# Filters by row halves, context by head columns, one output product per chunk, and statistics between normalisations in a four-layer kernel

## The chip, the cores and the metric

One core of one Trainium2 chip runs the whole program. The metric is device microseconds (us) of one execution. TensorE is PE in the rows, VectorE is DVE, ScalarE is ACT, GpSimd is POOL, and SyncE, which here only issues DMAs, is SP.

## What is computed

The input x is (32, 16, 16, 32) in fp32: 32 images of 256 tokens with 32 channels. Four blocks follow each other. Each adds a token mixer and then a second mixer to x, each behind a layer norm over the 32 channels. Cut to what the change touches:

```python
# block 0: linear attention, 4 heads of 32
q = softmax(q, over the 32 channels of a head) / sqrt(32)
k = softmax(k, over the 256 tokens)
context = einsum('bnhd,bnhe->bhde', k, v / 256)
x = x + layernorm(einsum('bhde,bnhd->bnhe', context, q) @ w_out + b_out) * ln_scale
# block 0: spectral unit (STU): causal convolution over tokens with 16 filters phi,
# weights M_phi_plus and M_phi_minus (the latter with alternating signs), scaled by sigma**0.25,
# plus three direct taps M_u, for four sequence lengths, weighted by a gumbel softmax
x = x + stu(layernorm(x))
# block 1: triangle update
a = sigmoid((x @ Wa1 + ba1) * (x @ Wa2 + ba2)); b likewise
x = x + sigmoid(x @ Wg + bg) * (layernorm(einsum('bikc,bkjc->bijc', a, b)) @ Wz + bz)
# blocks 1 and 3: recurrent cell behind a batch normalisation of Wx
x = x + scan(y = sigmoid(batchnorm(x @ W.T) + y @ V.T))
# blocks 2 and 3: row scan with a width-9 convolution; block 2: mixture of 16 experts, top 8
```

## The kernel before, in words

Channels of four images fill the 128 partitions (`NQ` = 4 groups of `C` = 32). The free axis holds `G` = 8 images of `T` = 256 tokens, 2048 columns, which are worked in `CH` = 4 chunks of 512 columns (`BANK`), the width of one of the eight PSUM banks. Everything is fp32, and a matmul leaves two records in the trace. Every engine has its own program, written out by hand in the order in which it runs, and counting semaphores tie them together: `wait_ge(S(name), n)` holds the engine and everything behind it. `keep_busy(n, k)` on PE issues n matmuls of 512 columns whose results nobody reads.

**Layer norm** (`ln_centre`, `ln_square`, `ln_spread`, `ln_rstd`): PE subtracts the mean (L197), ACT squares (L256), PE averages the squares (L203), ACT takes Ln and Exp (L262, L267), and DVE multiplies (L281, L1142, L1242, L1326). `ln_pe` interleaves the chunks.

**Attention** runs over U = 16 units, a chunk j and a group q each. Its loops are software pipelines. On PE, turn i issues `attn_proj(i)` (k and q, 512 columns each, and v, four matmuls of 128 columns), `attn_mid(i-1)` (four transposes, L567), one call of `filters` if there is one, `attn_ctx(i-2)` (four matmuls 128x128 of 128 columns, L578), `attn_out(i-3)` (two matmuls of 256 columns onto the 32 partitions of group q) and a second call of `filters`. `filters(m)` makes two columns e of the STU's filters, from a strided weight of 128 rows, 256 columns each, into bank 1; there are 16 calls, two each in turns 5 to 12 (`FILT_FROM` = 5). It waits until ACT has copied the call before (`filt_sb`). On DVE, turn i does `v_k(i)` (maximum, L1093), `v_q(i)` (L1100, L1102, L1106), `v_qw(i-1)` (L1111, L1113, L1116) and `v_ctx(i-2)` (L1121 and four small multiplications on L1129, one for each head, since only the diagonal blocks of the 128x128 product are wanted). ACT does `a_k(i)` (L910), `a_kn(i-1)` (L931), a copy of filters (L939), `a_v(i)` (L919), `a_q(i)` (L925), another copy of filters, and `a_y` (L935) when a chunk's four groups are out. POOL multiplies q by its weight (L457). Only when all 16 units are through does the layer norm of the output start. k alternates between banks 0 and 5.

**STU**: SP's DMAs spread the filters over `toep`, then PE convolves (L622). `add_stu(j)` adds a bank to x in 16 small steps (L1165), which also turn token-major rows into channel groups.

**Triangle**: `twice` writes the normalised x into `xm` in token order and into `xnH` in row order. PE takes columns of both as weights: `xnH[:, m]` is contiguous, `xmQ[:, :, m]` has a stride of 16 elements. Then DVE adds biases (L1198) and multiplies (L1203), ACT takes the sigmoids (L978, L982) and, with DVE, spreads `a` over a block diagonal (L987, L1208), and PE multiplies (L687). `add_triangle` brings the result back.

**Recurrent cells** (`rnn(0, 4)` and `rnn(1, 8)`): PE makes Wx per chunk (`wx`), then `BUSY_BN[0]` = 3 unread matmuls, then waits for `bn_mean_in`. DVE writes the guessed state with four memsets (L1253, L1254), takes four batch statistics (L1258) and aggregates them (L1259).

## Time and profile before

| | |
|---|---|
| median of 3 runs | 501.35 us (499.7 to 503.72) |
| the profiled execution's own time | 500.5 us |
| its span, first to last instruction | 498.7 us |
| mean granted clock of TensorE, share of full | 0.974 |
| PE busy | 460.4 us (92%) |
| weight loads | 290.6 us (58%) |
| DVE busy | 264.7 us (53%) |
| ACT busy | 180.4 us (36%) |
| POOL busy | 32.6 us (7%) |

The span is one execution recorded by the hardware profiler. Busy shares are averages over the stages: attention (about 23 to 137 us), its STU (to 267), the triangle (to 309), the first cell (to 346), row scan, experts and row scan (to 462), the second cell and the store (to 499). Matmul records overlap, so a stage with PE at 99% is bound by PE's order of issue and not by its peak.

### The profile page before, as it was taken

To read this page: it belongs to the slowest core of one execution; us is meant where nothing else is said; L and a number is where in the kernel's file an instruction comes from. 1 tells how busy PE (TensorE), PEld (TensorE's weight loads), DVE (VectorE), ACT (ScalarE), POOL (GpSimd) and SP (SyncE) were. 2 spreads that over 40 slices of the span, in tenths; PEclk is the share of its full clock that TensorE was granted. 3 is DMA by queue.
4 is the path that set the end of the run, shared out by engine and by line. 5 is a ranking of instruction groups with operands and counts; after the bars stand their busy time and mean duration, and the time that the engine had idled before them with its cause. 6 is when DMAs were issued, how large, how long until landed. Compare 5 with 4: busy or idle time off the path is not lost.

```text
span 498.7 us, 6421 instructions
## 1 busy us (share of the span) xinstructions
PE 460.4 (92%) x2488; PEld 290.6 (58%) x2488; DVE 264.7 (53%) x566; ACT 180.4 (36%) x362; POOL 32.6 (7%) x32
## 2 busy tenths in 40 slices
PE   6999999998879999998998998998999899999991
PEld 2456677765327476753764855485475575475490
DVE  3599878787579140105105645646533736633745
ACT  1785766663650000001002272454504510504360
POOL 0135221123000000000000000000000000000000
PEclk8999999998999999999999999998999988999996
DMA  9300000059940000000002000000000000000003
GB/s 276 152 2 1 1 0 1 1 128 224 197 85 0 2 0 0 1 0 0 1 2 41 1 1 1 1 1 2 0 1 2 1 0 1 0 2 1 0 1 85
DMA packets 6506, 15.20 MB, mean 30 GB/s; under 512 B 2619, under 2 KB 5323, under 8 KB 5707
## 3 DMA queue, kind: packets, MB, share of 16 engines
q1 hardware_dynamic: 5899, 14.25, 11.7%
q10 hardware_dynamic: 576, 0.52, 0.3%
q8 instruction: 20, 0.33, 0.3%
q14 instruction: 11, 0.09, 0.1%
HBM read 5.86 MB, written 1.05 MB: 14 GB/s over the span
## 4 chain that ended last, share of the span: by engine, by line
PE 67%; DVE 19%; ACT 8%; issue 4%; DMA 1%; POOLq 0%; SPq 0%; DVEq 0%; ACTq 0%
PE bank L510 22%; PE bank L622 19%; PE bank L791 5%; PE bank L203 5%; PE bank L736 3%; PE bank L747 3%; PE bank L197 3%; DVE xQ L1165 2%; ACT lnv L262 2%; PE bank L219 2%; PE bank L578 1%; ACT rs L267 1%; DVE attn_scratch L1129 1%; ACT sq L256 1%; DVE xn L249 1%
## 5 line engine op out<-in xcount | busy, mean ns | idle before, releaser
L622 PE MATMUL bank<-xn,arena 128*128 128x512 f32 (+15 forms) x332 | 88.9, 427 | 2.4 <-DVE xn L249 2.4
L622 PEld LDWEIGHTS bank<-xn,arena 128*128 128x128 f32 x332 | 56.3, 190 | 36.0 <-issue 27.0
L256 ACT ACTIVATE sq<-bank 128x512 f32<-128x512 f32 x36 | 21.3, 591 | 119.5 <-PE bank L197 98.6
L510 PE MATMUL bank<-sb_consts 128*128 128x512 f32 (+1 forms) x140 | 62.5, 571 | 0.0
L1165 DVE TENSOR_TENSOR xQ<-bank,xQ 32x128 f32<-32x128 f32 x64 | 24.5, 382 | 33.1 <-PE bank L656 18.0
L203 PE MATMUL bank<-sq,sb_consts 128*128 128x512 f32 x72 | 38.4, 615 | 0.9
L510 PEld LDWEIGHTS bank<-sb_consts 128*128 128x128 f32 x140 | 25.3, 194 | 23.3 <-issue 23.1
L262 ACT ACTIVATE lnv<-bank 128x512 f32<-128x512 f32 x36 | 21.5, 598 | 33.6 <-PE bank L203 33.6
L510 PE MATMUL bank<-xn,sb_w_attn 128*128 128x512 f32 x64 | 31.1, 604 | 0.6 <-DVE attn_scratch L1106 0.5
L1174 DVE TENSOR_TENSOR arena<-bank,rs 128x512 f32<-128x512 f32 x4 | 2.8, 692 | 51.7 <-ACT rs L267 51.7
L791 PEld LDWEIGHTS bank<-arena,sb_w_late 128*128 128x128 f32 x180 | 23.0, 191 | 11.1 <-DVE arena L1332 8.0
L791 PE MATMUL bank<-arena,sb_w_late 128*128 128x128 f32 x180 | 27.2, 287 | 1.7 <-DVE arena L1332 1.3
L736 PE MATMUL bank<-arena,sb_consts 128*128 128x128 f32 x144 | 27.7, 276 | 0.7 <-DVE arena L1282 0.7
L747 PE MATMUL bank<-arena,sb_w_late 128*128 128x128 f32 x144 | 27.9, 276 | 0.0
L197 PE MATMUL bank<-xQ,sb_consts 128*128 128x512 f32 x40 | 22.0, 643 | 6.2 <-DVE xQ L1165 3.3
L203 PEld LDWEIGHTS bank<-sq,sb_consts 128*128 128x128 f32 x72 | 12.1, 190 | 22.6 <-ACT sq L256 11.5
L1016 ACT ACTIVATE arena<-bank 128x128 f32<-128x128 f32 x72 | 20.0, 278 | 14.0 <-PE bank L747 13.8
L457 POOL TENSOR_TENSOR attn_scratch<-attn_scratch 128x512 f32<-128x512 f32 x16 | 20.3, 1271 | 71.3 <-DVE attn_scratch L1116 71.3
L267 ACT ACTIVATE rs<-lnv 128x512 f32<-128x512 f32 x36 | 22.7, 631 | 1.1
L736 PEld LDWEIGHTS bank<-arena,sb_consts 128*128 128x128 f32 x144 | 21.7, 192 | 2.3 <-issue 2.3
L1332 DVE SCALAR_TENSOR_TENSOR arena<-bank,xn 128x128 f32<-128x128 f32 x30 | 8.8, 292 | 26.7 <-PE bank L791 25.9
L747 PEld LDWEIGHTS bank<-arena,sb_w_late 128*128 128x128 f32 x144 | 21.9, 192 | 0.2
(191 smaller groups left out, 690.2 us busy)
## 6 DMA issues: line engine op xcount, KB each, us to landing
arena<-arena SPq DMA_DIRECT2D x4, 1024.0 KB, 16.5
arena<-in_w_spec SPq DMA_DIRECT2D x2, 1024.0 KB, 9.5
arena<-arena SPq DMA_DIRECT2D x4, 512.0 KB, 8.2
sb_w_late<-in_w_late SPq DMA_DIRECT2D x1, 1100.5 KB, 12.6
xR<-in_x SPq DMA_DIRECT2D x4, 256.0 KB, 4.4
arena<-arena SPq DMA_DIRECT2D x4, 256.0 KB, 4.1
sb_w_attn<-in_w_attn SPq DMA_DIRECT2D x1, 641.0 KB, 6.7
arena<-arena SPq DMA_DIRECT2D x4, 128.0 KB, 2.5
```

The costliest lines, as they stand in the source:

```text
L197: pe.matmul(bank[:, i % CH, :], centre, src, start=True, stop=True).then_inc(S("ln_centred"), 1)
L203: pe.matmul(bank[:, var_bank(i), :], mean32, sq[:, i % 2, :], start=True, stop=True)\
L256: act.activation(sq[:, i % 2, :], bank[:, i % CH, :], ACT.Square).then_inc(S("ln_squared"), 1)
L262: act.activation(lnv[:, i % 2, :], bank[:, var_bank(i), :], ACT.Ln, bias=LN_EPS[i // CH])\
L267: act.activation(rs[:, i % 2, :], lnv[:, i % 2, :], ACT.Exp, scale=-0.5).then_inc(S("ln_rstd"), 1)
L457: link(pool.tensor_tensor(qn[:, u % 3, :], qe[:, u % 2, :], qw[:, u % 2, :], ALU.mult))
L510: return mm(ps, lhsT, rhs, start=True, stop=True)
L622: return mm(bank[:, k, lo * B:hi * B], lhs, cols[:, at * B:(at + hi - lo) * B], start=start, stop=stop, **kw)
L736: mm(place(s, h), ident, z_[:, h, s % RES, :, :], start=True, stop=False)
L747: mm(place(s_, h), rvt[i], before(h, s_ % RES), start=False, stop=True)\
L791: last = mm(bank[:, 4 + h % 2, 0:P], band[i][:, w, :], carry[:, h - 1, w:w + 4, :], start=(w == 0), stop=(w == 2))
L1165: last = dve.tensor_tensor(xs, stu[C * r:C * r + C, :, G * q:G * q + G].rearrange("p t g -> p g t"), xs, ALU.add)
```

## The change

- `filters`: the weight rows are laid twice, in partitions 0 to 63 and 64 to 127, so that each of the two matmuls of a call uses 64 rows and a bank of its own (4 and 5). The calls start one turn earlier, and the first of a turn stands between k and q. The loads of `w_stu` and `w_spec` become six DMAs each. sigma's powers are made for all rows, with four small copies in place of one, and POOL scales phi in two instructions in place of three.
- `attn_ctx`: 16 matmuls of 32 columns, each onto its head's 32 partitions, in place of four of 128; `v_ctx` is one multiplication.
- `attn_out`: once for each chunk, eight matmuls that alternate over the four groups of 32 partitions; `qn` has six buffers, `cwt` eight.
- k uses bank 0 alone, v bank 1. DVE does `v_qw(i-1)` ahead of `v_q(i)`.
- `BUSY_DRAIN`: one unread matmul in turns 13 to 16. The layer norm of the first chunks of the output starts in turns 16 and 17.
- the STU's last chunk: one copy, 16 matmuls that regroup rows, and one addition replace 16 small additions; two single `keep_busy` replace one of six.
- `xm` is kept column-major (w, g, h), so that both sets of weights of the triangle are contiguous, and `add_triangle` follows.
- `rnn`: POOL writes the guessed state; in the first cell two batch statistics stand between the normalisations, in the second cell one; `BUSY_BN[0]` is 1.

```diff
-WX_EARLY = [0, 2]
-FILT_FROM = 5
+WX_EARLY = [1, 2]
+FILT_FROM = 4
+BUSY_DRAIN = 1
+BUSY_STU = 1
+FILTER_ROWS = [(at + to, rows) for at in (0, 64)
+               for to, rows in ((0, slice(0, KF)), (KF, slice(64, 64 + AR)), (KF + AR, slice(KF + AR, 64)))]
+QN = 6
-BUSY_BN = (3, 1, 2)
+BUSY_BN = (1, 1, 2)
...
-            load("w_stu_in", w_stu[:, :], d["w_stu"])
...
+            for to, rows in FILTER_ROWS:
+                load("w_stu_in", w_stu[to:to + rows.stop - rows.start, :], d["w_stu"][rows, :])
+            for to, rows in FILTER_ROWS:
+                load("w_spec_in", wm_raw[to:to + rows.stop - rows.start, :, :].rearrange("p f m -> p (f m)"), d["w_spec"][rows, :])
...
+            def guess(i):
+                for h in range(2):
+                    link(pool.memset(y_[:, h, RES - 1, 1:PASS + 1, :], 0.5))
+                    link(pool.memset(y_[:, h, RES - 1, 0:1, :], 0.0))
+                pool.sem_inc(S("y_guess"), 1)
+            guess(0)
             add_states(0)
+            pool.wait_ge(S("x_back"), 2 * CH)
+            guess(1)
             add_states(1)
...
-                for e in (2 * m, 2 * m + 1):
-                    last = full(bank[:, 1, (e % 2) * T:(e % 2 + 1) * T],
-                                wm_raw.rearrange("p f (d e) -> p (f d) e", e=C)[:, :, e], phi_cols)
+                for half in range(2):
+                    rows = slice(64 * half, 64 * half + 64)
+                    last = full(bank[:, 4 + half, 0:T],
+                                wm_raw.rearrange("p f (d e) -> p (f d) e", e=C)[rows, :, C // 2 * half + m], phi_cols[rows, :])
...
-                if u >= 2:
-                    pe.wait_ge(S("k_exp"), u - 1)
-                full(bank[:, 5 * (u % 2), :], wk[:, q, :], flat(xn, j)).then_inc(S("k_ps"), 1)
+                if u >= 1:
+                    pe.wait_ge(S("k_exp"), u)
+                full(bank[:, 0, :], wk[:, q, :], flat(xn, j)).then_inc(S("k_ps"), 1)
+                for m in filter_turn(u, 0):
+                    filters(m)
...
-                    for h in range(2):
-                        i = 2 * g + h
-                        last = mm(bank[:, 6, g * P:(g + 1) * P], kN[:, u % 2, i * P:(i + 1) * P],
-                                  vo[:, u % 2, i * P:(i + 1) * P], start=(h == 0), stop=(h == 1))
+                    for half in range(2):
+                        for h in range(HEADS):
+                            cols = slice((2 * g + half) * P + C * h, (2 * g + half) * P + C * h + C)
+                            last = mm(bank[C * h:C * h + C, 6, g * C:(g + 1) * C], kN[:, u % 2, cols], vo[:, u % 2, cols],
+                                      start=(half == 0), stop=(half == 1))
...
+            def attn_out(j):
+                pe.wait_ge(S("ctx_sb"), NQ * (j + 1))
+                pe.wait_ge(S("q_norm"), NQ * (j + 1))
                 if j >= 1:
                     pe.wait_ge(S("attn_y"), j)
                 for g in range(2):
+                    for q in range(NQ):
+                        u = NQ * j + q
+                        last = full(bank[C * q:C * q + C, 7, g * T:(g + 1) * T], cwt[:, u % (2 * NQ), g, :],
+                                    qn[:, u % QN, g * T:(g + 1) * T])
                 last.then_inc(S("attn_ps"), 1)
...
+                if U - 4 < i <= U:
+                    pe.wait_ge(S("filt_sb"), C // 2)
+                    keep_busy(BUSY_DRAIN, 4)
+                if i >= 3 and (i - 3) % NQ == NQ - 1:
+                    attn_out((i - 3) // NQ)
                 for m in filter_turn(i, 1):
                     filters(m)
+                if i == U:
+                    centre_y(0)
+                if i == U + 1:
+                    pe.wait_ge(S("filt_sb"), C // 2)
+                    centre_y(1)
+                    ln_spread(pe, CH)
+            centre_y(2)
+            ln_spread(pe, CH + 1)
+            centre_y(3)
+            ln_spread(pe, CH + 2)
+            ln_spread(pe, CH + 3)
...
-            keep_busy(BUSY[3], 6)
+            keep_busy(BUSY_STU, 6)
+            pe.wait_ge(S("stu_rows"), 1)
+            for r in range(NQ):
+                for q in range(NQ):
+                    last = full(bank[C * q:C * q + C, 3, r * P:(r + 1) * P], ident[:, C * r:C * r + C],
+                                both.rearrange("p (n b) -> p n b", b=B)[:, :, G * q:G * q + G])
+            last.then_inc(S("stu_cols"), 1)
+            keep_busy(BUSY_STU, 6)
             pe.wait_ge(S("x_stu"), CH)
...
-                            else xmQ.rearrange("p g (h w) -> p (g h) w", w=W)[:, :, m])
+                            else xm[:, m * P:(m + 1) * P])
...
+            centre_cols(3)
+            ln_spread(pe, CH * LN_RNN + 2)
+            wx(0, LN_RNN, 0)
+            ln_spread(pe, CH * LN_RNN + 3)
...
+            for at, sign in ((0, 1.0), (32, -1.0), (64, 1.0), (96, -1.0)):
+                last = act.activation(odd_sig4[at:at + 32, :], sig4[at:at + 32, :], ACT.Copy, scale=sign)
+            last.then_inc(S("sig4"), 1)
...
             for i in range(U + 2):
                 if i < U:
                     v_k(i)
-                    v_q(i)
                 if 0 <= i - 1 < U:
                     v_qw(i - 1)
+                if i < U:
+                    v_q(i)
...
-                for out_ in (tokens(xmQ, j).rearrange("p g (h w) -> p g h w", w=W), h4):
+                for out_ in (xm.rearrange("p (w g h) -> p g h w", w=W, g=G)[:, :, 4 * j:4 * j + 4, :], h4):
...
-            add_stu(3)
+            dve.wait_ge(S("stu_ps"), CH)
+            dve.tensor_copy(both, bank[:, 7, :]).then_inc(S("stu_rows"), 1)
+            dve.wait_ge(S("stu_cols"), 1)
+            x3 = tokens(xQ, 3).rearrange("p g (n r) -> p g n r", r=NQ)
+            dve.tensor_tensor(x3, bank[:, 3, :].rearrange("p (r n g) -> p g n r", r=NQ, g=G), x3, ALU.add).then_inc(S("x_stu"), 1)
...
+            normalise_cols(0)
+            normalise_cols(1)
+            statistics(0, 0)
+            normalise_cols(2)
+            statistics(0, 1)
+            normalise_cols(3)
```

## Rows read from the trace of the kernel before

**Rows 1.** Busy by stretch: us, PE, PEld, DVE, ACT, POOL, clock, DMA share, GB/s

```profile
48.00:105.00 57.00, 56.63 (x289) 42.54 (x289) 44.24 (x99) 39.61 (x78) 10.45 (x9) 1.00 0.01 3
...
121.00:127.00 6.00, 5.91 (x21) 3.15 (x20) 2.39 (x11) 0.23 (x1) 1.27 (x1) 0.72 1.02 201
```

**Rows 2.** Timeline of DVE, unit 4 of attention, and k maxima of units 0, 5, 13

```profile
23.54 0.69 DVE L1093 TENSOR_REDUCE attn_scratch<-bank 128x2 f32<-128x512 f32 x1 [0.52 <-PE bank L510]
...
42.47 0.69 DVE L1093 TENSOR_REDUCE attn_scratch<-bank 128x2 f32<-128x512 f32 x1
...
45.17 0.70 DVE L1111 TRANSPOSE_TENSOR_REDUCE attn_scratch<-attn_scratch 128x16 f32<-128x512 f32 x1
...
46.99 0.92 DVE L1129 TENSOR_TENSOR attn_scratch<-bank,attn_scratch 32x64 f32<-32x64 f32 x4
47.94 0.69 DVE L1093 TENSOR_REDUCE attn_scratch<-bank 128x2 f32<-128x512 f32 x1
...
102.99 0.69 DVE L1093 TENSOR_REDUCE attn_scratch<-bank 128x2 f32<-128x512 f32 x1 [1.39 <-PE bank L510]
```

**Rows 3.** Timeline of PE, one unit with two calls of filters

```profile
59.36 1.88 PE L510 MATMUL bank<-xn,sb_w_attn 128*128 128x512 f32 x4
61.08 1.05 PE L510 MATMUL bank<-wvo,xn 128*128 128x128 f32 x8
...
62.41 1.15 PE L510 MATMUL bank<-sb_w_stu,arena 128*128 128x256 f32 x4
63.40 1.05 PE L578 MATMUL bank<-attn_scratch 128*128 128x128 f32 x8
64.38 1.05 PE L510 MATMUL bank<-attn_scratch 128*32 128x256 f32 x4
65.36 1.26 PE L510 MATMUL bank<-sb_w_stu,arena 128*128 128x256 f32 x4
66.46 1.88 PE L510 MATMUL bank<-xn,sb_w_attn 128*128 128x512 f32 x4
```

**Rows 4.** Timeline of ACT, the same unit, and an early small step

```profile
20.92 0.20 ACT L897 ACTIVATE nsig<-sig 32x1 f32<-32x1 f32 x1
...
65.04 0.62 ACT L925 ACTIVATE attn_scratch<-attn_scratch 128x512 f32<-128x512 f32 x1
66.66 1.06 ACT L939 ACTIVATE arena<-bank 128x512 f32<-128x512 f32 x1 [0.99 <-PE bank L510]
```

**Rows 5.** Timeline, end of attention: DVE's last units, ACT, last addition

```profile
119.67 0.71 DVE L1111 TRANSPOSE_TENSOR_REDUCE attn_scratch<-attn_scratch 128x16 f32<-128x512 f32 x1
...
126.77 0.69 ACT L935 ACTIVATE xR<-bank,sb_w_attn 128x512 f32<-128x512 f32 x1 [8.31 <-PE bank L510]
...
136.48 0.75 DVE L1144 SCALAR_TENSOR_TENSOR xQ<-xn,sb_w_attn,xQ 128x512 f32<-128x512 f32 x1
```

**Rows 6.** Timeline of PE and its weight loads in the triangle

```profile
272.74 3.65 PEld L510 LDWEIGHTS bank<-sb_w_late,xR 128*128 128x128 f32 x32 [0.99 <-issue]
...
276.30 7.06 PEld L510 LDWEIGHTS bank<-sb_w_late,arena 128*128 128x128 f32 x32
...
305.73 3.70 PE L510 MATMUL bank<-arena,sb_w_late 128*32 128x128 f32 x128 [0.25 <-ACT arena L1002]
```

**Rows 7.** Timeline of DVE and PE, last chunk of the STU, and regrouping

```profile
260.67 6.33 DVE L1165 TENSOR_TENSOR xQ<-bank,xQ 32x128 f32<-32x128 f32 x16 [18.02 <-PE bank L656]
...
267.06 1.13 PE L197 MATMUL bank<-xQ,sb_consts 128*128 128x512 f32 x2 [1.27 <-DVE xQ L1165]
...
380.79 1.08 PE L510 MATMUL bank<-arena,sb_consts 128*32 128x128 f32 x32
```

**Rows 8.** Groups by line and shape: busy us, mean ns | idle before, releaser

```profile
L249 DVE TENSOR_TENSOR xn<-bank,rs 128x512 f32<-128x512 f32 x12 | 12.6, 1047 | 8.3 <-ACT rs L267 8.3
```

**Rows 9.** Timeline of DVE, second recurrent cell, last normalisation and aggregation

```profile
462.60 0.69 DVE L1326 TENSOR_TENSOR arena<-bank,rs 128x512 f32<-128x512 f32 x1 [2.27 <-ACT rs L267]
...
466.68 0.26 DVE L1259 BATCH_NORM_AGGREGATE arena<-arena 128x2 f32<-128x24 f32 x1
```

More of the change, by code:

```diff
@@ L557, in attn_proj @@
                 for i in range(4):
[L558 removed]
+                    last = full(bank[:, 1, i * P:(i + 1) * P], xn[:, j * BANK + i * P:j * BANK + (i + 1) * P],
                                 wvo[:, q, :])
@@ L909, in a_k @@
                 for g in range(2):
-                    last = act.activation(kE[:, u % 2, g * T:(g + 1) * T], bank[:, 5 * (u % 2), g * T:(g + 1) * T], ACT.Exp,
+                    last = act.activation(kE[:, u % 2, g * T:(g + 1) * T], bank[:, 0, g * T:(g + 1) * T], ACT.Exp,
                                           bias=nkm[:, 2 * u + g:2 * u + g + 1],
```

139 lines of the change are left out of this document (63 added, 76 removed).

## Prediction

> **What bounds the kernel now.** I read the busy shares by stretch first, then the timelines of three engines through one attention unit, then the places where the change edits the chain. In 48 to 105 us PE is busy for 56.63 of 57.00 us and DVE for 44.24 [rows 1]. So attention has two regimes. Without filters a unit of DVE lasts from one k maximum to the next, 47.94 - 42.47 = 5.47 us, with no idle time in between: DVE is the bound [rows 2]. With two calls of filters PE takes 66.46 - 59.36 = 7.10 us for a unit: k and q 1.72, v and the transposes 1.33, filters 0.99, context 0.98, output 0.98, filters 1.10 [rows 3]. That stretch, from the maximum at 47.94 to that at 102.99, lasts 55.05 us for 8 units [rows 2]. After attention the chain runs through single waits: the drain of the pipeline, the last chunk of the STU, the triangle's weight loads and the batch statistics. The reader should see in each row what starts the next one; a step off that chain gives nothing. The sum is made against the profiled execution, 500.5 us, which is 0.85 us under the median of the runs.
>
> **Start of attention.** ACT makes four small copies instead of one ahead of the weight that unit 0 waits for. A copy took 0.20 us [rows 4], three more are 0.6, of which 0.1 is slack: +0.5 us. SP issues nine more small DMAs ahead of `w_late`; that tile is first used in the triangle, 270 us in, so its later issue is hidden, and the filter weights are wanted only when ACT scales them in turn 1. If they came late, ACT's k, v and q behind that wait would be held; I put 0 to 1 us there and take 0.
>
> **Units without filters.** The four small multiplications took 0.92 us; one with as many columns costs a quarter, 0.23 [rows 2]. DVE's unit falls to 5.47 - 0.69 = 4.78 us. PE's own work, k and q 1.72, v and transposes 1.33, context and output (below), is less than that. With k in one bank, PE's k(u+1) waits until ACT has read k(u). The maximum stands first in DVE's turn, so this wait ends some 2 us into a unit of 4.78: hidden. Putting the q weights ahead of `v_q(i)` gives PE that much longer to bring q. The first filter call of turn 4 needs POOL's last sum of weights, which comes when that turn is under way, and q(4) and v(4) are queued behind it: +1 us. The last four units carry an unread matmul of 0.86 and, in one of them, the whole output product, so PE holds them at 5.05 each. Before, the five units ahead of the filters took 47.94 - 23.54 = 24.4 us and the three behind them 119.67 - 102.99 = 16.7 [rows 2, 5]. Those 41.1 us become 38.6 (four units of 4.78, less 1.7 since the first turns lack the steps for earlier units, as before, where five took 3.0 less than 5 x 5.47; then 1.0; then four of 5.05): -2.5.
>
> **Units with filters.** Here the length is a loop that crosses engines. A call waits until ACT has copied the call before, so from the end of one copy: filters, q 0.86, v and transposes 1.33, context, filters, the copy 1.06 [rows 3, 4], and 0.2 of hand-overs. k runs beside the copy. Two prices are missing.
>
> *Filters by halves.* The trace has no matmuls on different rows at once. Its nearest rows are those on different columns: 128 records with 128 columns in 3.70 us, 0.029 each, while contiguous full weights took 3.65 for 32, 0.114 each [rows 6]. Four tiles ran together, weight loads included. Strided weights took 7.06 for 32, 0.22 each [rows 6]. So two halves together cost two loads and matmuls in sequence instead of four: 0.5, with 0.15 to change the tile shape 0.65. The other end is no overlap: 0.99, up to 1.10. I take 0.65, because loads and matmuls of different column tiles overlap.
>
> *Context.* 32 records of 32 columns. At the rate of the 128-column tiles they cost 0.93, as much as the 0.98 of now; by the column count a quarter, 0.23, with 0.12 for the change of shape 0.35. No row has a sustained rate above 0.029, so I take 0.75, nearer that end.
>
> The loop is then 0.65 + 0.86 + 1.33 + 0.75 + 0.65 + 1.06 + 0.25 = 5.55 us. Two turns hold an output product of 1.0: 8 x 5.55 + 2.0 = 46.4 against 55.05, -8.6 us. DVE at 4.78 and ACT, whose work in such a unit I add to about 4.5, are both under that. The output product itself goes from 0.98 in each unit to 1.0 in four, because four groups of 32 partitions run at once [rows 6].
>
> A filter unit goes from two changes of tile shape to five. The call of filters behind the column-tiled output takes 1.10, the one behind the transposes 0.99 [rows 3], so a change costs of the order of 0.1; the sum has it for most of them, and 0.3 a unit more is in the upper end. The Trainium skill, page TensorEngine Tiling (Array Packing), section Key Properties, says that changing the tiling mode drains TensorE; by that, each of the five costs something, and the trace agrees with its 0.1.
>
> The context's 0.75 lies between 0.35 and 0.98 by rows alone. The Trainium skill, page TensorE: Matmul & The Clock Gate, section Back-to-back issue gap, gives about 25 ns as the floor for matmuls of 1 to 64 columns. By it, 32 records are 0.80 as an estimate, and 0.92 with the change of shape would make the loop 0.17 us longer.
>
> **Drain and first layer norm.** Before, from the end of DVE's unit 15 at 119.67 to the end of the last addition at 136.48 + 0.75 took 17.6 us [rows 5]; ACT's last copy of the output starts at 126.77, and the clock was 0.72 in 121 to 127 [rows 1, 5]. After, PE comes last: two contexts 1.5, an unread matmul 1.0, two centrings and a spread 2.7, the output 1.0, 6.2 in all. The weight of the last q, three steps of DVE with 1.7 us [rows 2] and one of POOL, ends before that. Then ACT is last, with the copy 0.7, two squares, and Ln and Exp of three chunks, eight passes of 512 columns like the copy of q, 0.6 each [rows 4, 5]: 5.9 with hand-overs. Then DVE's two steps, 0.7 and 0.75. That is 14.2 with 0.6 of gaps: -3.4. The toeplitz DMAs start as the filters end, some 14 us earlier, and the convolution that needs them starts 14 us earlier too: unchanged. Attention in all: +0.5 - 2.5 - 8.6 - 3.4 = -14.0 us.
>
> **Last chunk of the STU.** From 260.67 to the centring at 267.06, 6.4 us [rows 7]. Now a copy 0.69, 16 matmuls like those that took 1.08 for the same 32 records [rows 7], an addition 0.69 and three hand-overs of 0.15: 2.9. Gain 3.5. The unread matmuls lie beside DVE's work.
>
> **Triangle.** The weights with stride took 7.06, the contiguous ones 3.65 [rows 6]: -3.4 on PE, of which DVE, which must first finish the biases and product of a, passes on 3.2. ACT's sigmoid of b and its part of the block diagonal follow at once. The write of `xm` gets a stride of 512 bytes. A 512-column multiplication with a strided output took 1.05, the usual one 0.69 [rows 2, 8]: +0.35 for the one on the chain. Sum -2.9. The new order in `add_triangle` is worth -0.1 to +0.35 a step, beside PE's work: 0.
>
> **Cells.** In the second cell 466.68 - 463.29 = 3.4 us lie between the last normalisation and the aggregation: four memsets and four statistics of one pass of 512 columns, 0.7 each [rows 9]. Three statistics are left: 2.2 us, so -1.2. One unread matmul hides under it; three would have ended 1.5 later, so this cut is needed for the gain. In the first cell the two statistics lie inside a layer norm in which ACT is busy: wx(0) delays the last spread by 0.6 and the second statistic the last normalisation by 0.7. Of 1.5 gained 0.85 is left. POOL's memsets follow its edges by 1 us, and nobody wants the guess for 8 us: 0.
>
> **Sum.** -14.0 - 3.5 - 2.9 - 0.85 - 1.2 = -22.4 us: 478.1 for a profiled execution, 479 beside the median. I say 479.5, since hand-overs that I left out can only add.
>
> **Rivals.** (1) *The halves don't overlap.* 16 calls at 1.0 instead of 0.65, all inside the loop: +5.6 to +7, 486. For it: no row here has two row tiles at work, and the loads are strided. Against it: rows 6. 0.22. (2) *Context at its column count.* The loop is 0.4 shorter and the last units reach 4.8: 475. 0.10. (3) *Slower than before: the clock.* The new units have PE waiting in every loop, and its columns are fewer. Where PE stood still in the drain, the mean granted clock of 121 to 127 fell to 0.72, so part of it ran at 1.2 GHz and not at 2.4 [rows 1]. If that happened in attention, each unit's PE work of about 4.5 us would double. The gain of 22.4 is gone when five of the 16 units run like that, and seven give 510. Against it: the mean of the whole run is 0.974, row scans with their short bursts and waits included. 0.04. (4) *Another engine takes over.* If ACT in the loop waits for v or q in the new order, units stay near 6.3: 485. 0.07. The forecast keeps 0.54, and 0.03 is for losses elsewhere that cancel the gain. Range: 473 takes in rival 2, 490 rivals 1 and 4 with the upper ends of context and tile changes. About 1% (5 us) is what a measurement of this kernel can tell from no change: faster 0.93 (all but rival 3 and that remainder), same 0.04, slower 0.03.
>
> **What the profile after would show.** Units with filters 5.6 us apart (right), 6.5 (rival 1); a context burst of 0.75; units 0 to 3 at 4.8; the last x addition of attention near 123; the STU's centring 3 us behind the end of its convolution; weight loads of the triangle equal in both halves; aggregation 2.2 behind the last normalisation. The forecast is wrong above all if the granted clock dips inside attention or if the loop through ACT is not the one that I wrote.

## The result and the profile after

The changed kernel took 484.5 us, the median of four runs (481.3 to 485.1), beside 500.5 for the kernel before on the same chip (498.4 to 503.7): a ratio of 0.967 with a 95% interval of 0.961 to 0.973. A later series gave 485.7 against 501.5, 0.966 (0.961 to 0.970). So the gain is 16 us; 479.5 us was forecast, inside 473 to 490. The profiled execution of the changed kernel, 481.3 us with a span of 479.3, is the fastest of its runs, and that of before was near its median, so the two profiles differ by 19.2 us and not by 16. Why is told with the clock below.

The page of the kernel after, shares and the chain that ended last:

```profile
PE 433.3 (90%) x2896; PEld 263.7 (55%) x2896; DVE 250.3 (52%) x496; ACT 179.1 (37%) x365; POOL 32.9 (7%) x39
...
PEclk9998899999999999999999999998999999999996
...
PE bank L648 20%; PE bank L520 16%; PE bank L836 5%; PE bank L210 5%; DMA arena<-in_w_spec 4%; PE bank L781 3%; PE bank L792 3%; PE bank L204 3%; PE bank L226 2%; ACT lnv L269 2%; ACT rs L274 1%; DVE xn L256 1%; DVE xQ L1217 1%; ACT arena L986 1%; SPq L420 1%
```

The reader should see two things here. The transfer of `w_spec` is on the chain, and the fifth of the forty slices (48 to 60 us), inside attention, has a clock of 8 tenths, like the fourth ahead of it.

The timeline of DVE in the kernel after, its maxima of k (one for each unit of attention) and the last addition:

```profile
24.52 0.69 DVE L1147 TENSOR_REDUCE attn_scratch<-bank 128x2 f32<-128x512 f32 x1 [1.20 <-PE bank L520]
...
37.95 0.68 DVE L1147 TENSOR_REDUCE attn_scratch<-bank 128x2 f32<-128x512 f32 x1
42.60 0.68 DVE L1147 TENSOR_REDUCE attn_scratch<-bank 128x2 f32<-128x512 f32 x1
52.62 0.69 DVE L1147 TENSOR_REDUCE attn_scratch<-bank 128x2 f32<-128x512 f32 x1 [1.47 <-PE bank L520]
58.42 0.69 DVE L1147 TENSOR_REDUCE attn_scratch<-bank 128x2 f32<-128x512 f32 x1 [0.99 <-PE bank L520]
...
127.45 0.75 DVE L1196 SCALAR_TENSOR_TENSOR xQ<-xn,sb_w_attn,xQ 128x512 f32<-128x512 f32 x1
```

A unit without filters lasts 42.60 - 37.95 = 4.65 us (before 5.47 [rows 2]), one with filters 58.42 - 52.62 = 5.80 (before 7.10 [rows 3]). Between the two stands unit 4, from 42.60 to 52.62, 10.0 us. The maximum of unit 12 is at 94.59, so the eight units with filters took 51.99 us where those of before took 55.05 [rows 2].

The timeline of PE in the kernel after, in unit 4 and later in one undisturbed unit:

```profile
44.41 1.23 PE L520 MATMUL bank<-sb_w_stu,arena 64*128 64x256 f32 x4 [2.76 <-POOLq L477]
45.57 2.07 PE L520 MATMUL bank<-xn,sb_w_attn 128*128 128x512 f32 x2
47.44 1.91 PE L520 MATMUL bank<-wvo,xn 128*128 128x128 f32 x8
...
76.98 0.82 PE L520 MATMUL bank<-sb_w_stu,arena 64*128 64x256 f32 x4 [0.42 <-ACT arena L986]
77.72 1.12 PE L520 MATMUL bank<-xn,sb_w_attn 128*128 128x512 f32 x2
78.69 1.05 PE L520 MATMUL bank<-wvo,xn 128*128 128x128 f32 x8
79.58 0.60 PE L580 MATMUL bank<-sb_consts,attn_scratch 128*128 128x128 f32 x4
80.11 0.46 PE L592 MATMUL bank<-attn_scratch 128*32 128x32 f32 x32
80.50 0.82 PE L520 MATMUL bank<-sb_w_stu,arena 64*128 64x256 f32 x4
```

PE stands still for 2.76 us ahead of the first filters, until POOL's queue releases it. Then the product with v takes 1.91 us instead of 1.05: a half-speed clock. In the undisturbed unit a call of filters takes 77.72 - 76.98 = 0.74 us and the whole context 80.50 - 80.11 = 0.39, and PE waits for ACT's copy of the call before (0.42).

Who held it, in the timeline of POOL:

```profile
41.87 2.35 POOL L475 TENSOR_TENSOR arena<-arena 128x1024 f32<-128x1024 f32 x1 [0.18 <-POOL attn_scratch L459]
```

And in that of ACT:

```profile
28.91 2.19 ACT L995 ACTIVATE arena<-arena,fw 128x1024 f32<-128x1024 f32 x2 [0.69 <-DMA arena<-in_w_spec]
...
80.22 0.60 ACT L978 ACTIVATE attn_scratch<-bank 128x512 f32<-128x512 f32 x1 [0.53 <-PE bank L580]
80.71 0.59 ACT L966 ACTIVATE attn_scratch<-bank 128x512 f32<-128x512 f32 x1
81.20 0.62 ACT L972 ACTIVATE attn_scratch<-attn_scratch 128x512 f32<-128x512 f32 x1
81.72 1.02 ACT L986 ACTIVATE arena<-bank 128x512 f32<-128x512 f32 x1
```

POOL's last of three sums ends at 44.2. ACT's scaling of the spectral weights waits for `w_spec`, whose last piece now has nine more issues ahead of it. The issues explain little of that: SP had issued all of `w_spec` at 4.99 us before and at 8.17 after. The transfers are slower. The GB/s rows of the two pages, first the kernel before, in slices of 12.5 and 12.0 us:

```profile
GB/s 276 152 2 1 1 0 1 1 128 224 197 85 0 2 0 0 1 0 0 1 2 41 1 1 1 1 1 2 0 1 2 1 0 1 0 2 1 0 1 85
GB/s 220 133 93 1 1 1 1 1 211 222 200 29 0 1 0 0 1 0 0 1 0 46 0 1 3 0 1 2 1 0 2 2 0 1 0 1 1 0 1 90
```

Both kernels move some 5.3 MB here, but the one after needs a third slice. From 12 to 16 us it moves 148 GB/s where the one before moved 437, with the DMA engines about as busy (0.93 and 1.03). Its `w_spec` comes in pieces of 16, 3 and 45 rows instead of over all 128 partitions at once; that this is the reason is likely and not tested.

The last four rows of ACT give the loop of a filter unit: after the transposes ACT copies k, v, q's exponential and the second call's result, and only then may PE start the next call.

After attention, the rows that answer to [rows 6, 7, 9], from the timelines of PE and, below them, of DVE in the kernel after:

```profile
254.63 1.05 PE L204 MATMUL bank<-xQ,sb_consts 128*128 128x512 f32 x2
...
264.17 3.74 PE L520 MATMUL bank<-sb_w_late,arena 128*128 128x128 f32 x32
```

```profile
253.81 0.69 DVE L1246 TENSOR_TENSOR xQ<-bank,xQ 128x512 f32<-128x512 f32 x1 [1.21 <-PE bank L520]
...
292.18 1.13 DVE L1295 TENSOR_TENSOR xQ<-xQ,arena 128x512 f32<-128x512 f32 x1
...
444.60 0.69 DVE L1387 TENSOR_TENSOR arena<-bank,rs 128x512 f32<-128x512 f32 x1 [1.73 <-ACT rs L274]
445.21 2.15 DVE L1307 BATCH_NORM_STATS2 arena<-bank 128x6 f32<-128x512 f32 x3
447.39 0.26 DVE L1320 BATCH_NORM_AGGREGATE arena<-arena 128x2 f32<-128x24 f32 x1
```

The addition of the last STU chunk is one step of 0.69 us where there were sixteen of 6.33 in all, its centring starts at 254.63, the matmuls on the second half of the triangle's weights take 3.74 us, and these are loaded as fast as the first, the aggregation comes 447.39 - (444.60 + 0.69) = 2.1 us behind the end of the last normalisation, and the update of the triangle has a step of 1.13 us that took 0.69 before.

Where the time went, by the same points of both profiles:

| point of the chain | before | after | change of the stretch |
|---|---|---|---|
| end of the last addition of attention | 137.23 | 128.20 | -9.03 |
| end of the convolution | 259.53 | 250.77 | +0.27 |
| last centring of the STU | 267.06 | 254.63 | -3.67 |
| first product of the block diagonal | 291.41 | 275.84 | -3.14 |
| aggregation, cell 1 | 322.38 | 306.68 | -0.13 |
| last normalisation ahead of cell 2 | 462.60 | 444.60 | -2.30 |
| aggregation, cell 2 | 466.68 | 447.39 | -1.29 |
| end of the span | 498.7 | 479.3 | -0.1 |

The -2.30 is the clock, not an edit: between the last normalisations of the two row scans the kernel before took 75.38 us (387.22 to 462.60), with a granted clock of 0.66 in 406 to 416, and the kernel after 72.76 (371.84 to 444.60) with 1.00 there, which is -2.6. The other +0.3, between the aggregation and 371.84, is open.

### The profile page after: what moved, and what is told of

It is laid out like the page before. It is cut to its first block, busy times and chain, and to the rows that moved or that the text cites. A ratio compares the mean times of both kernels' runs of the same rounds, so it can differ in the third digit from the quotient of the medians.

```text
span 479.3 us, 7157 instructions
## 1 busy us (share of the span) xinstructions
PE 433.3 (90%) x2896; PEld 263.7 (55%) x2896; DVE 250.3 (52%) x496; ACT 179.1 (37%) x365; POOL 32.9 (7%) x39
## 3 DMA queue, kind: packets, MB, share of 16 engines
HBM read 5.86 MB, written 1.05 MB: 14 GB/s over the span
## 4 chain that ended last, share of the span: by engine, by line
PE 62%; DVE 17%; ACT 9%; DMA 4%; issue 4%; SPq 1%; POOL 1%; POOLq 0%; DVEq 0%; ACTq 0%
PE bank L648 20%; PE bank L520 16%; PE bank L836 5%; PE bank L210 5%; DMA arena<-in_w_spec 4%; PE bank L781 3%; PE bank L792 3%; PE bank L204 3%; PE bank L226 2%; ACT lnv L269 2%; ACT rs L274 1%; DVE xn L256 1%; DVE xQ L1217 1%; ACT arena L986 1%; SPq L420 1%
## 5 line engine op out<-in xcount | busy, mean ns | idle before, releaser
L520 PE MATMUL bank<-sb_consts 128*128 128x512 f32 (+1 forms) x132 | 59.1, 564 | 0.0
L520 PE MATMUL bank<-xn,sb_w_attn 128*128 128x512 f32 x64 | 35.6, 650 | 4.6 <-ACT attn_scratch L957 3.1
L520 PEld LDWEIGHTS bank<-sb_consts 128*128 128x128 f32 x132 | 23.0, 190 | 19.1 <-issue 18.9
L1226 DVE TENSOR_TENSOR arena<-bank,rs 128x512 f32<-128x512 f32 x4 | 4.1, 1037 | 51.4 <-ACT rs L274 51.4
L836 PEld LDWEIGHTS bank<-arena,sb_w_late 128*128 128x128 f32 x180 | 23.0, 191 | 11.1 <-DVE arena L1393 8.0
L1217 DVE TENSOR_TENSOR xQ<-bank,xQ 32x128 f32<-32x128 f32 x48 | 18.3, 382 | 14.9 <-PE bank L648 14.3
L520 PEld LDWEIGHTS bank<-wvo,xn 128*128 128x128 f32 x128 | 17.7, 200 | 8.2 <-issue 8.2
```

The costliest lines, as they stand in the source:

```text
L520: return mm(ps, lhsT, rhs, start=True, stop=True)
L836: last = mm(bank[:, 4 + h % 2, 0:P], band[i][:, w, :], carry[:, h - 1, w:w + 4, :], start=(w == 0), stop=(w == 2))
L1217: last = dve.tensor_tensor(xs, stu[C * r:C * r + C, :, G * q:G * q + G].rearrange("p t g -> p g t"), xs, ALU.add)
```

## The experiments

All times are medians, each beside the kernel before on the same chip. The three series had the kernel before at 501.8, 501.4 and 501.5 us, so they can be compared; the changed kernel is 484.5 or, in the third series, 485.7.

### The clock, and the changed kernel once more

Edit: none.

> The changed kernel itself once more, on the chip of the three below. 481 to 486 us (its median was 484.5). What it tells: whether the half-speed clock behind the stall of turn 4 (44 to 51 us of the span) is there in another execution, and whether the one in the experts' part, which its first profile lacked, comes in others. If the two windows of some 7 us are what the times differ by, the profile of an execution near 485 has a window more than that of 481.3.

Measured: 485.66 us (480.27 to 486.48, six runs), ratio 0.966 (0.961 to 0.970). Busy time by stretch in the profile of that kernel, an execution of 484.2 us (columns as in [rows 1]):

```profile
44.00:52.00 8.00, 7.53 (x60) 4.87 (x60) 3.87 (x8) 4.35 (x9) 1.27 (x1) 0.79 0.01 2
224.00:232.00 8.00, 7.51 (x15) 3.36 (x16) 0.42 (x2) 1.12 (x2) 0.00 (x0) 0.79 0.00 0
...
392.00:400.00 8.00, 8.00 (x54) 5.61 (x54) 1.37 (x4) 1.88 (x2) 0.00 (x0) 0.57 0.01 2
```

The same stretches in the first profile, of 481.3 us:

```profile
44.00:52.00 8.00, 7.59 (x56) 5.08 (x56) 3.31 (x7) 3.51 (x9) 1.48 (x2) 0.58 0.01 2
224.00:232.00 8.00, 5.99 (x15) 2.96 (x16) 1.90 (x5) 1.26 (x3) 0.00 (x0) 1.00 0.00 0
...
392.00:400.00 8.00, 7.88 (x59) 4.75 (x59) 3.54 (x13) 1.88 (x2) 0.00 (x0) 1.00 0.01 2
```

The execution of 484.2 finished attention 1.5 us sooner (126.7 against 128.2) and still ended later: it lost its clock near 228 us and in the experts near 396, and the first one did not. So stretches at half speed come and go between executions of one kernel and are worth 1 to 3 us each, which is as much as most differences between the medians here.

### Is turn 4 the loss, and what of it is the clock?

```
-FILT_FROM = 4
+FILT_FROM = 5
```

> The first filter call moves from turn 4 to turn 5 (FILT_FROM back to 5), nothing else. Theory A (the stall of turn 4 is the wait for POOL's third sum of weights, and the half-speed clock of the 6.8 us behind it is a result of that stall): POOL's sum ends at 44.2 us, turn 5 starts later than that, so PE doesn't stand still, no clock window lies near 44 to 51 us, the maximum of k that stood at 52.62 comes some 4 us earlier against its neighbour, and the whole is 3 to 4.5 us faster than the changed kernel (about 481 beside its median of 484.5, 477 for a profile like the one of 481.3). Rival B (the clock window comes for another reason, for instance every first block of short column-tiled matmuls): only the 2.8 us of idle time go, the clock window of some 7 us moves along with the first filters, and the gain is at most 1.5 us. Rival C (turns with filters are limited by ACT's chain of copies and a later start only moves work into the drain): no gain.

Measured: 479.91 us (478.88 to 481.92), ratio 0.959 (0.954 to 0.964): 4.6 to 5.7 less than the changed kernel. The maxima of units 3 to 6 are at 38.11, 42.76, 47.40 and 52.05 us, 4.65 apart; the mean clock of 43 to 53 us is 1.00; attention ends at 124.19 instead of 128.20, 4.0 us earlier. Theory A holds, with a gain slightly above its 3 to 4.5.

```
                 if m == 0:
+                    keep_busy(3, 5)
                     pe.wait_ge(S("phi_cols"), 1)
```

> Three unread matmuls of 512 columns (0.86 us each, 2.6 together) stand ahead of the wait for POOL's sum in turn 4; the wait itself stays. Theory A (the clock falls because PE stood still for 2.76 us): PE's idle time ahead of the first filter call becomes under 0.5 us, the clock window of 43.8 to 50.7 us is gone, and of the 4.2 us lost in unit 4 the part that came from the clock, 1.2 to 2 us, comes back. Rival B (the clock falls anyway): the window stays, and the time is that of the changed kernel within 0.5 us.

Measured: 481.42 us (477.58 to 483.86), ratio 0.958 (0.951 to 0.965). The wait stays and costs PE nothing visible any more, in the timeline of PE of this kernel:

```profile
40.91 2.74 PE L520 MATMUL bank<-sb_consts 128*128 128x512 f32 x6
43.85 0.82 PE L520 MATMUL bank<-sb_w_stu,arena 64*128 64x256 f32 x4 [0.20 <-POOLq L477]
...
45.56 1.05 PE L520 MATMUL bank<-wvo,xn 128*128 128x128 f32 x8
```

The product with v takes 1.05 us, not 1.91, and the mean clock from 38 to 60 us is 1.00. Unit 4 lasts 7.26 us. So the wait for POOL costs 7.26 - 5.80 = 1.5 us, and the clock behind it the rest: unit 4 was 10.0 in the first profile and 8.88 in the control, 1.6 to 2.8 us. Theory A holds, at somewhat more than it expected. PE's stall isn't a sufficient cause in every execution, though: of the eight profiles with a stall of 2.75 us or more ahead of the first filters, seven show the low clock behind it and one, that of the whole context below, with 3.40 us of stall, does not. None of the five without the stall shows one there.

```
-            for to, rows in FILTER_ROWS:  load("w_stu_in", ...)
             for to, rows in FILTER_ROWS:  load("w_spec_in", ...)
+            for to, rows in FILTER_ROWS:  load("w_stu_in", ...)
```

> The six loads of w_spec are issued ahead of the six of w_stu; nothing else. Theory A (ACT's first scaling of the spectral weights waits for w_spec, and POOL's three sums follow it one by one, so that its late end at 44.2 us starts with the nine more DMA issues): w_spec arrives some 1.5 to 2.3 us earlier, the third sum ends near 42.5, the stall of PE in turn 4 shrinks from 2.8 us to about 1, and the kernel is 0.7 to 2.5 us faster than the changed one. Rival B (POOL's sums are paced by the q products that stand between them, one for each turn): the sums stay 5 us apart, the end moves by under 0.5 us, no gain; since w_stu now comes later, the softmax of the filter weights, which DVE works out ahead of unit 0, may then hold DVE by up to 1 us.

Measured: 491.20 us (490.74 to 494.72), ratio 0.982 (0.976 to 0.989): 6 to 7 us slower than the changed kernel. Rival B had this wait, at up to 1 us; neither theory had its size. The timeline of DVE in this kernel:

```profile
29.02 0.16 DVE L1131 TENSOR_TENSOR fw<-sb_w_stu 128x4 f32<-128x4 f32 x1 [8.88 <-DMA sb_w_stu<-in_w_stu]
...
34.35 0.69 DVE L1147 TENSOR_REDUCE attn_scratch<-bank 128x2 f32<-128x512 f32 x1 [2.15 <-PE bank L520]
```

The softmax of the filter weights waits 8.88 us for `w_stu`, ACT's queue has sigma's step and the copies of `wvo` behind it, and unit 0 starts at 34.35 instead of 24.52. POOL's sums then begin at 42.22, 47.11 and 51.77, about 4.8 us apart as in rival B, and the stall of unit 4 stays (9.85 us for that unit). The transfers, not their issues, set the time: SP issued `w_stu` only 2.4 us later than before the edit, and DVE waited for it 8.9 us.

```
-FILT_FROM = 4                       (and one unread matmul of the drain less)
+FILT_FROM = 6
-                if i in (1, 2):     ACT scales the spectral weights in turns
+                if i in (2, 3):
-                if u < FRACS - 1:   POOL adds them behind q_normalise(u)
+                if 1 <= u < FRACS:
```

> ACT scales the spectral weights in turns 2 and 3 instead of 1 and 2, POOL adds them one turn later, the first filter call comes in turn 6 instead of 4 (one unread matmul of the drain goes with it). Theory A (two waits cost time at the start of attention: the late arrival of w_spec, for which ACT stands with the k and v of unit 1 behind it, and POOL's sum in turn 4): both waits are gone, units 0 to 5 are 4.65 us apart throughout, and the kernel is 1 to 3 us faster than with the first call in turn 5 alone (479.9), so 477 to 479. Rival B (the end of the filters, some 6 us later, now holds the drain, since the unread matmuls and the second centring wait for the last copy of a filter, or the toeplitz transfers come too late for the convolution): as fast as or up to 3 us slower than with turn 5.

Measured: 478.74 us (476.28 to 479.56), ratio 0.956 (0.952 to 0.961). The DMA wait of ACT is gone, the maxima of units 3 to 6 are at 36.82, 41.48, 46.12 and 50.77, and attention ends at 122.05, 2.1 us before that of the run with turn 5. Theory A holds in the trace; the time is 1.2 lower, less than the scatter of the clock.

### Do the halves overlap?

```
-                    rows = slice(64 * half, 64 * half + 64)
+                    rows = slice(0, 64)
```

> Both halves of a filter call read weights and columns from partitions 0 to 63, so that their matmuls use the same rows of the array and can't run beside each other; as many instructions, the same output since both halves of the partitions hold the same data. Theory A (the halves overlap in the changed kernel, which is why a call takes 0.74 to 0.80 us): a call takes 1.0 to 1.1 us here, a unit with two filter calls 6.3 to 6.5 us instead of 5.8, and the kernel is 4 to 7 us slower than the changed one. Rival B (the halves do not overlap; the shorter time of a call is from contracting over 64 rows): the call stays at 0.74 to 0.80 and the time within 1 us.

Measured: 487.46 us (487.24 to 491.20), ratio 0.975 (0.969 to 0.982). The timeline of PE of this kernel, one unit:

```profile
56.77 1.26 PE L520 MATMUL bank<-sb_w_stu,arena 64*128 64x256 f32 x4
57.96 1.13 PE L520 MATMUL bank<-xn,sb_w_attn 128*128 128x512 f32 x2
59.16 1.25 PE L520 MATMUL bank<-sb_w_stu,arena 64*128 64x256 f32 x4
```

A call takes 57.96 - 56.77 = 1.19 us instead of 0.74, and a unit 6.35 (52.77 to 59.12 in its maxima) instead of 5.80. Attention ends 4.4 us later than in the first profile of the changed kernel and 5.9 later than in the control. The medians differ by only 2 to 3 us, under the 4 to 7 expected. The overlap is shown; two halves on the same rows are even slower than the 0.99 that a whole call took before [rows 3].

### What is the context worth?

```
-  for half, for h:  mm(bank[C * h:C * h + C, 6, g * C:(g + 1) * C], kN[.. 32 columns], vo[.. 32 columns])
+  for half:         mm(bank[:, 6, g * P:(g + 1) * P], kN[.. 128 columns], vo[.. 128 columns])
   DVE: one tensor_tensor of 128x64 -> four of 32x64, as before
```

> The context goes back to four matmuls of 128 columns for each unit (0.98 us in the trace of before) with four small multiplications on DVE (0.92 us); all else stays as in the changed kernel. Theory A (the context's 0.38 and the one small multiplication carry most of the gain of attention): DVE's unit without filters becomes 4.65 + 0.69 = 5.3 us, the loop of a filter unit grows by 0.6 on PE to 6.4, so with 7 units without and 8 with filters some 4 + 4.5 = 8.5 us are lost, 6 to 10. Rival B (filter units are held by ACT and not by PE's loop, so that PE's longer context lies in its idle time): only the units without filters lose, 3 to 4.5 us.

Measured: 489.62 us (487.21 to 491.13), ratio 0.977 (0.972 to 0.982): 4 to 5 us slower than the changed kernel. The maxima of k from unit 4 on are at 43.83, 50.78, 57.05 and 64.32; a unit without filters lasts 5.5 to 5.6, one with filters 6.27. The timeline of ACT in this kernel shows how the 0.47 came in:

```profile
73.88 0.60 ACT L977 ACTIVATE attn_scratch<-bank 128x512 f32<-128x512 f32 x1 [0.54 <-PE bank L580]
74.84 0.60 ACT L965 ACTIVATE attn_scratch<-bank 128x512 f32<-128x512 f32 x1 [0.35 <-PE bank L591]
```

ACT's copy of v waits for the context that still reads the buffer of two units earlier. With a context of 0.39 us this wait isn't there, since ACT's copy of k takes longer. Both theories are half right: the units without filters lose 0.8 to 0.9 us, more than the 0.69 of A and B, and those with filters 0.47 and not 0.6 or nothing. The profiled execution ended attention at 133.09, 4.9 to 6.4 us later, although it lost no clock in unit 4.

### Which loop sets a filter unit?

```
                 full(bank[:, 2, :], wq[:, q, :], flat(xn, j)).then_inc(S("q_ps"), 1)
+                for m in filter_turn(u, 1):      (PE: was behind attn_out)
+                    filters(m)
...
                     a_k(i)
+                for m in filter_turn(i, 1):      (ACT: was behind a_q)
+                    a_filters(m)
```

> In the changed kernel, the second filter call of a turn moves ahead: on PE from behind the output product to right behind q, on ACT from behind q's exponential to right behind k's. Number and form of the instructions are the same. Theory A (the loop that sets the 5.80 us of a filter unit is: filter call, q, v, transposes on PE, then ACT's copies of the transposes and of v, q's exponential and the second filter copy, 3.16 + 2.45 + 0.2; the context lies beside ACT's copies, in no loop): with the second copy taken out of that loop the unit falls to PE's own work of some 5.1 us, or ACT's of 4.7, so 5.1 to 5.4, and the kernel is 3 to 5 us faster than the changed one, 480 to 481.5. Rival B (my prediction's loop: one copy of filters, then filters, q, v, transposes, context, filters; the order on ACT doesn't matter): the unit stays at 5.8 and the time within 1 us. Rival C (the second call now waits on PE for ACT with q and v behind it): slower, units of 6 us and more.

Measured: 482.74 us (481.15 to 485.52), ratio 0.964 (0.959 to 0.968), beside 485.66 for the control. In its profile attention ends at 126.94 where the control had 126.69, but its first maximum came at 25.64 and not at 24.53: from there on it is 0.9 us shorter. On top of the later first call:

> The same move of the second filter call on top of the first call in turn 6 with the later scaling of the spectral weights (478.7 us). Theory A: both gains add, 8 units of some 5.2 us and 7 of 4.65 us, the last addition of attention near 118.5 us of the span instead of 122.1, and 474.5 to 476.5 us. Rival (the drain is held by the end of the filters, or the toeplitz transfers become late): 477 to 479.

Measured: 477.37 us (475.83 to 478.82), ratio 0.951 (0.948 to 0.954). This is the fastest version, 8.3 us under the control of the same series. Beside 478.74 without the early second call, its trace shows no gain in attention: it ends at 122.65, and at 122.05 there. The two differ by one thing more, an unread matmul in turn 13, which only this version still has. Counted from the maximum of unit 0, it is 0.2 us ahead at that of unit 13 (67.52 against 67.70) and 0.5 behind at that of unit 14 (74.05 against 73.53). The timeline of PE in this kernel, one unit:

```profile
68.96 1.13 PE L520 MATMUL bank<-xn,sb_w_attn 128*128 128x512 f32 x2
70.17 0.81 PE L520 MATMUL bank<-sb_w_stu,arena 64*128 64x256 f32 x4
70.92 1.16 PE L520 MATMUL bank<-wvo,xn 128*128 128x128 f32 x8
...
72.83 1.13 PE L520 MATMUL bank<-xn,sb_w_attn 128*128 128x512 f32 x2
73.89 0.82 PE L520 MATMUL bank<-sb_w_stu,arena 64*128 64x256 f32 x4
```

And ACT's copy of the first call, in its timeline:

```profile
69.08 1.04 ACT L986 ACTIVATE arena<-bank 128x512 f32<-128x512 f32 x1 [0.60 <-PE bank L520]
```

No idle time is marked on PE any more, and the unit lasts 5.68 us (56.97 to 62.64 and on in its maxima), the same with the first call in turn 4 (5.67). Theory A's 5.1 to 5.4 is wrong, for two reasons. k, which used to take 0.86 [rows 3], takes 73.89 - 72.83 = 1.06 behind the column tiles. And q takes 70.17 - 68.96 = 1.21 between two calls of filters, but part of that is a wait: ACT's copy ends at 69.08 + 1.04 = 70.12, the second call starts at 70.17, and all eight second calls of this profile start 0.05 to 0.06 us behind such an end. So rival C had the wait, but not its size. The old loop, through the second copy, did set the 5.80, since taking that copy out of it shortens the unit; a new loop, from the second call through k and the first call to ACT's copy, sets the 5.68. If q alone took 1.06 like k, PE's own work would be about 5.5 (an estimate), 0.3 us under the 5.80. What the edit gains is 0.12 a unit, 1 us in 8 units. The rest of the 2.9 us between the medians of the control and of the early call in turn 4 isn't in attention.

### The batch statistics

```
-BUSY_BN = (1, 1, 2)
+BUSY_BN = (3, 1, 2)
```

> Three unread matmuls instead of one ahead of PE's wait for the mean of the batch statistics, in both cells. Theory A (my prediction: the cut is needed for the gain, since three of them end later than DVE's shortened statistics): the product with the mean starts up to 1.5 us after the aggregation in each cell, so the kernel is 1.5 to 3 us slower than the changed one. Rival B (the wx matmuls end early enough, or PE would stand still): within 0.5 us, or a little faster if the filled wait keeps the clock up at the start of a scan.

Measured: 484.65 us (483.97 to 485.61), ratio 0.968 (0.964 to 0.973): no difference in the medians. The timeline of DVE in this kernel, cell 2:

```profile
449.03 0.26 DVE L1320 BATCH_NORM_AGGREGATE arena<-arena 128x2 f32<-128x24 f32 x1
450.91 0.16 DVE L1324 COPY arena<-bank 128x1 f32<-128x1 f32 x1 [1.61 <-PE bank L520]
```

From the aggregation to the copy of the mean it is 1.88 us, and 1.96 in cell 1; in the changed kernel 0.81 (447.39 to 448.20). The cut is worth 1.1 us in a cell by the trace, as theory A says, and the 2.2 us don't show in the time of four runs. The steps of the trace decide here; the medians can't.

### The update of the triangle

```
-  scalar_tensor_tensor(out=flat(upd, k), in0=bank[:, k, :], in1=flat(gate, k))
-  tensor_tensor(xc, xc, flat(upd, k).rearrange("p (j n) -> p n j", j=4))
+  scalar_tensor_tensor(out=grid_cols(upd), in0=bank[:, k, :].rearrange("p (j n) -> p n j", j=4), in1=grid_cols(gate))
+  tensor_tensor(xc, xc, grid_cols(upd))
```

> The update of the triangle is computed and stored as before, in the order of the grid columns, so that the second step (addition to x) reads all its operands in the same order; only these two instructions for each chunk differ. Theory A (the second step lasts 1.05 to 1.13 us instead of 0.69 because it reads with a stride of 512 bytes, and delays the first normalisation by some 0.9 us): the second step is 0.69 again, the four chunks are through 5.7 us after the start instead of 7.1, and the aggregation of cell 1 comes 0.4 to 1.0 us sooner after the first chunk than in the changed kernel. Rival B (ACT's steps of the layer norm hold that stretch anyway): the second step is shorter, the aggregation moves by under 0.2 us. In the time either is near the limit of what five rounds can show.

The gate is read here in an order that doesn't match the new order of `xm`, so the update has the wrong gate for most elements; the shapes and the steps are the same. Measured: 483.33 us (480.40 to 484.37), ratio 0.964 (0.960 to 0.968), 1.2 us under the changed kernel and inside the scatter. The second step takes 0.69 us, the four chunks are through at 296.87, 5.6 after the start, and the aggregation comes 306.04 - 291.23 = 14.8 us behind the first update instead of 306.68 - 291.40 = 15.3. A gain of 0.5 was to be had from the order. The first step reads PSUM with the same stride of 512 bytes here and still takes 0.74 to 0.75 us, as in the changed kernel: on the PSUM operand the stride costs nothing. To have the gain with the right gate, ACT must write the gate in grid order, here on top of the fastest version:

```
-  act.activation(gate[:, :], bank[:, 0:4, :], ACT.Sigmoid, bias=bg)
+  act.activation(gate.rearrange("p (n k j) -> p k j n", k=4, j=4), bank[:, 0:4, :].rearrange("p k (j n) -> p k j n", j=4), ACT.Sigmoid, bias=bg)
```

> On top of that, ACT writes the gate of the triangle in the order of the grid (its sigmoid of 2048 columns took 1.96 us), and the update of the triangle is computed and stored in that order as before, so that no step of DVE reads with a stride of 512 bytes: its second steps take 0.69 instead of 1.05 to 1.13 us. Theory A (ACT writes with a stride at the same rate): the aggregation of cell 1 comes 0.6 us sooner after the first update, as in the run with the old update, and the kernel is 0.3 to 0.8 us faster, which five rounds may not show in the time but the trace does. Rival B (ACT's strided write of the gate takes longer, up to 3 us): the copy of z for the transposes, which follows on ACT, comes later by that, and up to 1 us is lost.

Measured: 479.11 us (478.18 to 480.06), ratio 0.954 (0.951 to 0.957), 1.7 slower than the same kernel without it. The timeline of ACT:

```profile
271.81 3.76 ACT L1045 ACTIVATE arena<-bank,sb_w_late 128x2048 f32<-128x2048 f32 x1
```

It took 1.95 us at 271.79 in the kernel without the edit. The 1.8 us more delay the first update by 1.6, of which the shorter steps give back 0.5. Rival B holds: of the two engines that can take the stride, DVE loses 0.5 us on the chain and ACT 1.6.

## Why the prediction was right, and where its terms were off

The forecast of a gain came true, inside the range and 5 us short, and most stages behaved as written. Two of its steps did not, and they are the two that it named as signs of being wrong: the clock dipped inside attention, and the loop of a filter unit is not the one that I wrote. That the number held is partly luck. The clock hit one unit and not five, and the wrong loop came near in length because the context was counted too long. By its own steps, against the trace:

- **Units without filters** (4.78 forecast): 4.65. The first four took 18.1 us where 17.4 were counted without the wait, the difference being ACT's wait for `w_spec`, which I had put at 0 with 0 to 1 open. The run with the later scaling removed it (17.15). What made `w_spec` late, the slower transfers, I had not priced at all.
- **Turn 4's wait for POOL, "+1 us"**: this is the term that was mis-sized most. Unit 4 took 10.0 us, 4.2 more than its neighbour and 3.5 more than its forecast share of 5.55 + 1.0: 1.5 for the wait, and up to 2.8 for the clock that fell behind it. Rival 3 had the mechanism, a clock lost in attention, but priced it for five to seven units or nothing. One unit was the case that came. With the first call moved, the median falls by 4.6 to 5.7 us, as much as the gap to the forecast; the trace shows 4.0 of them in attention.
- **Filters by halves** (0.65): 0.74. They overlap, shown by the run with both halves on the same rows; rival 1 is refuted.
- **Context** (0.75): 0.39, the low end that rival 2 stood for. It brought nothing of rival 2's 4 us, since the context isn't in the loop. The rule of the Trainium skill, page TensorE: Matmul & The Clock Gate, section Back-to-back issue gap, a floor of about 25 ns for 1 to 64 columns, would make 32 matmuls 0.80 us; here 32 records on four column tiles took 0.39, 12 ns each, so the measurement speaks against it for tiles that run at once.
- **The loop of a filter unit** (5.55): 5.80. The length is nearly right, the path isn't. With the measured prices of a call (0.74) and of the context (0.39) the loop that I wrote would be 5.37. I had PE's transposes, context and second call in it, and it goes from the transposes to ACT's copies of k, v and q's exponential and of the second call. The run with the whole context shows the path (ACT's v waits), that with the early second call shows that it gives way to another loop at 5.68. Rival 4 had ACT in the loop, but with a wait for v or q that the trace doesn't show, and at 6.3. What I had called 0.1 for a change of tile shape is 0.11 for q behind a call of filters (78.69 - 77.72 = 0.97 instead of 0.86) and 0.20 for k behind column tiles.
- **Last units and drain**: 19.9 and 13.75 us, forecast 20.2 and 14.2. The sum of the units is right and its parts aren't: I had four of 5.05, and the first two took 4.65 each, so the unread matmul was hidden there, and the one with the output product 5.79.
- **Attention**: -9.0 instead of -14.0. Of the 5.0 us lost, 3.5 are in unit 4, 1.1 in the other seven filter units, 0.7 in the first four and 0.5 in a later start than counted; the last units and the drain give 0.8 back.
- **STU's last chunk** -3.67 (forecast -3.5) and **triangle** -3.14 (-2.9): right.
- **Cell 1** -0.13 instead of -0.85. The step that failed is "-0.1 to +0.35 a step, beside PE's work: 0" of the triangle's update: the second step costs 0.36 to 0.44 more each, and DVE had no cover for them. 0.5 of the 0.7 is shown by the run with the old order; the other 0.2 stays open.
- **Cell 2** -1.29 (forecast -1.2), and the cut of unread matmuls was needed for it by the trace.
- **The clock elsewhere**: -2.3 in the profile, in no edit. Without it the profile would have shown -17 us, about what the medians show.

## What to carry to other kernels

A wait that costs 1.5 us by itself can cost three or four, when the engine that stands still is TensorE and comes back at half the clock: price a stall with what follows it, and fill it or move its user one turn later. When an operation is made cheaper, first write down which queue releases the next step of the loop. The context shrank by 0.6 us, and in a filter unit only the 0.47 by which it had held ACT's copy of v was worth anything. And a trace of one execution settles steps of half a microsecond that medians of six runs, with clocks that come and go, can't.

## What the runs showed of the hardware that was not expected

- Four column tiles of 32 columns ran 32 matmul records in 0.39 us, 12 ns each. Two row tiles of 64 rows with strided weights ran a call in 0.74 us, and in 1.19 on the same rows.
- Behind a change of tile shape a product of 512 columns took 0.97 us (behind two row tiles) or 1.06 (behind column tiles) instead of 0.86.
- A stride of 512 bytes on the SBUF operand of a DVE addition made 0.69 into 1.05 to 1.13 us, and on the PSUM operand of the step ahead of it it changed nothing (0.74 to 0.75); a write with a stride of 64 bytes by ACT made 1.95 into 3.76 for 2048 columns.
- Behind a stall of PE of 2.8 us the granted clock was 0.50, that is 1.2 GHz, for some 3 to 7 us in seven executions, and it stayed at 1.00 in one with a stall of 3.4 us. What decides between the two isn't shown.
- With the same bytes in narrower pieces the DMA engines were as busy (0.93 against 1.03 from 12 to 16 us) and moved 148 GB/s instead of 437.
